# The second dispatch of a mixture-of-experts layer: GpSimd makes its taken blocks, last permutations and expert numbers in place of VectorE, and register loads are moved

## What is computed

```python
x = x + xattn(layernorm(x), ctx)                # W_q, W_kv, W_out, gamma, beta
t = layernorm(x)
probs = softmax(t @ Wg + bg)
top_v, top_i = top_k(probs, 2)                  # two experts per token
top_v = top_v / (top_v.sum() + 1e-6)
for e in range(8):
    h = silu(t @ W1[e] + b1[e]) * (t @ W3[e] + b3[e])      # 128 -> 512
    out = out + combine[..., e] * (h @ W2[e] + b2[e])       # 512 -> 128
x = x + out
```

## Time and profile before

| | before |
|---|---|
| median of 3 runs | 163.03 us (162.93 to 163.41) |
| the profiled execution | 163.78 us, span 161.7 us |
| busy: PE, DVE, ACT, POOL | 136.9, 103.7, 76.2, 75.3 us |
| chain that ended last | PE 66%, DVE 13%, DMA 7%, ACT 7% |

### The profile page before, as it was taken

How to read it: one execution, slowest core, us unless ns; L and a number is a source line. 1 busy time by engine, 2 the same in 40 slices (tenths; PEclk the granted TensorE clock), 3 DMA queues, 4 the chain that set the end, 5 groups by cost and what they waited for, 6 DMA issues and landing times.

```text
span 161.7 us, 3923 instructions
## 1 busy us (share of the span) xinstructions
PE 136.9 (85%) x1152; PEld 128.4 (79%) x1152; DVE 103.7 (64%) x324; ACT 76.2 (47%) x210; POOL 75.3 (47%) x93
## 2 busy tenths in 40 slices
PE   6788896999999999897899899999999999993000
PEld 6677785779998999886778799999999999992000
DVE  0536699989899967988769744535363544444084
ACT  3078356857464698700633335363544545363000
POOL 3630002946553685104810777777777763334000
PEclk9999999999999999999999999999999999999755
DMA  4899910020000001338751399888868868001553
GB/s 136 268 329 285 231 33 0 0 114 19 2 2 4 0 0 46 102 99 287 230 152 70 88 323 307 267 243 247 254 195 247 272 212 276 32 27 41 153 140 97
DMA packets 21597, 23.57 MB, mean 146 GB/s; under 512 B 2333, under 2 KB 14457, under 8 KB 21577
## 3 DMA queue, kind: packets, MB, share of 16 engines
q1 hardware_dynamic: 19968, 20.30, 41.9%
q0 software_dynamic: 1440, 2.95, 6.3%
q10 hardware_dynamic: 169, 0.08, 0.2%
HBM read 19.91 MB, written 3.41 MB: 144 GB/s over the span
## 4 chain that ended last, share of the span: by engine, by line
PE 66%; DVE 13%; DMA 7%; ACT 7%; issue 3%; POOL 1%; SPq 1%; ACTq 0%; POOLq 0%; DVEq 0%
PE psum L1261 26%; PE psum L1274 12%; PE psum L1308 8%; PE psum L1290 5%; DMA early<-in_L_xattn_W_kv_dram 4%; PE psum L1037 2%; PE psum L1039 2%; PE psum L1038 2%; DMA y_back<-y_scratch 2%; DVE prob L753 2%; DVE xn L1030 2%; DVE negmax L748 2%; PE psum L1248 2%; ACT g_room L569 2%; DVE x L1027 1%
## 5 line engine op out<-in xcount | busy, mean ns | idle before, releaser
L1261 PE MATMUL psum<-probT,w 128*128 128x128 f32 x368 | 45.5, 276 | 1.7 <-issue 1.1
L987 DVE SCALAR_TENSOR_TENSOR probT<-psum,bias_col,prob 128x128 f32<-128x128 f32 x92 | 26.0, 343 | 29.7 <-ACT prob L667 29.0
L1261 PEld LDWEIGHTS psum<-probT,w 128*128 128x128 f32 x368 | 43.0, 192 | 2.5 <-issue 2.0
L667 ACT ACTIVATE prob<-psum,bias_col 128x128 f32<-128x128 f32 x92 | 26.2, 368 | 36.0 <-PE psum L1261 36.0
L513 POOL DMA_INDIRECT g_room<-xf_scratch,idx x22 | 22.0, 1000 | 22.1 <-DVE idx L963 8.8
L488 POOL TENSOR_TENSOR prob<-prob,rowsum 128x1232 f32<-128x1232 f32 x8 | 18.0, 2249 | 22.6 <-DVE rowsum L744 22.6
L1274 PE MATMUL psum<-w,probT 128*128 x184 | 25.0, 279 | 0.1
L522 POOL DMA_INDIRECT y_scratch<-xnT,out_row x18 | 17.6, 979 | 13.6 <-DVE xnT L996 10.6
L1274 PEld LDWEIGHTS psum<-w,probT 128*128 128x128 f32 x184 | 22.6, 191 | 0.8 <-issue 0.6
L1308 PE MATMUL psum<-vo,probT 128*128 128x128 f32 (+1 forms) x160 | 19.3, 276 | 0.0
L1308 PEld LDWEIGHTS psum<-vo,probT 128*128 128x128 f32 (+1 forms) x160 | 18.5, 192 | 0.0
(11 more groups left out here) (166 smaller groups left out, 180.2 us busy)
## 6 DMA issues: line engine op xcount, KB each, us to landing
w<-in_L_ffn_W_dram SPq DMA_DIRECT2D x54, 256.0 KB, 3.8
early<-in_L_xattn_W_kv_dram SPq DMA_DIRECT2D x2, 512.0 KB, 7.2
y_back<-y_scratch SPq DMA_DIRECT2D x4, 256.0 KB, 3.7
x_sb<-in_x_dram SPq DMA_DIRECT2D x2, 256.0 KB, 5.3
early<-in_L_xattn_W_q_dram SPq DMA_DIRECT2D x1, 512.0 KB, 7.0
early<-in_L_xattn_W_out_dram SPq DMA_DIRECT2D x1, 512.0 KB, 9.5
early<-in_L_ffn_b_dram SPq DMA_DIRECT2D x1, 512.0 KB, 4.8
xf_scratch<-xf SPq DMA_DIRECT2D x2, 256.0 KB, 2.6
```

The costliest lines, as they stand in the source:

```text
L667: act.activation(silu[:, j % 2, c, :], psum[:, 2 * (j % 2), c * P:(c + 1) * P], ACT.Silu, bias=bias_col[:, 0, bass.ds(expert, 1), c]).then ...
L987: dve.scalar_tensor_tensor(out=hT[:, j % 2, c, :], in0=psum[:, 2 * (j % 2) + 1, c * P:(c + 1) * P], scalar=bias_col[:, 1, bass.ds(expert[j ...
L1261: ins = pe.matmul(psum[:, 2 * (j % 2) + a, c * P:(c + 1) * P], w13[:, j % WR, a, c * P:(c + 1) * P], xt[:, j % XR, :], start=True, stop=True)
```

## The change

POOL takes over four pieces. `taken_blocks` becomes 11 steps ahead of gather(1), each waiting for the one before, and `gone_blocks` 4 steps between gather(2) and gather(3); `last_perm` (2 steps) and `other_experts` (8 steps) stand between gather(4) and gather(5). They leave DVE, which waits for `taken_ok` ahead of `other_tiles`. DVE loads expert number 0 ahead of the first `idx` and numbers 1 to 4 between `gated(0)` and `other_tiles`; `out_row` is made later, behind `bias_down(1)`. PE loads its number between the halves of `up(j)`, and does `logits(2)` ahead of `up(0)`.

```diff
+            def taken_blocks():
...
+                step(pool.tensor_scalar(room_left[:, :], bounds[:, 0, :], -1.0, float(FULL * P), ALU.mult, ALU.add))
+                step(pool.tensor_scalar(room_left[:, :], room_left[:, :], 0.0, None, ALU.max))
+                step(pool.tensor_tensor(taken_e[:, :], blocks[:, :], room_left[:, :], ALU.subtract))
...
+                step(pool.tensor_tensor(taken_of[:, :], pair_taken[:, :, 0], pair_taken[:, :, 1], ALU.add))
+            def gone_blocks():
+
+                pool.wait_ge(perm_ok, 2)
+                step(pool.tensor_copy(floor_2[:, 0:FIRST * K], first_floors))
+                step(pool.tensor_tensor(gone[:, :], floor_2[:, 0:FIRST * K], taken_of[:, :], ALU.subtract))
+                step(pool.tensor_scalar(gone[:, :], gone[:, :], 0.0, float(2 * NT * P), ALU.is_lt, ALU.mult))
+                pool.tensor_tensor(floor_2[:, 0:FIRST * K], floor_2[:, 0:FIRST * K], gone[:, :], ALU.add).then_inc(taken_ok, 1)
...
+                pool.wait_ge(q_ok, 1)
+                pool.tensor_tensor(perm[:, pairs, :],
+                                   iota_q[:, :].rearrange("p (o q) -> p o q", o=1).broadcast_to([P, (T - FIRST) * K, P]),
+                                   q_of[:, FIRST:T, :].rearrange("p t (k o) -> p (t k) o", o=1).broadcast_to([P, (T - FIRST) * K, P]),
+                                   ALU.subtract).then_inc(p_perm, 1)
+                pool.wait_ge(p_perm, 1)
+                pool.tensor_scalar(perm[:, pairs, :], perm[:, pairs, :], 0.0, None, ALU.is_equal).then_inc(perm_2_ok, 1)
+
...
+                pool.wait_ge(base_ok, 1)
+                pool.tensor_tensor(end_e[:, :], base[0:1, :], padded[0:1, :], ALU.add).then_inc(p_eid, 1)
+                pool.wait_ge(p_eid, 1)
+                pool.tensor_tensor(end_e[:, :], end_e[:, :], taken_e[0:1, :], ALU.add).then_inc(p_eid, 1)
...
+                                   ALU.subtract).then_inc(p_eid, 1)
...
+                pool.tensor_scalar(ended[:, :, :], ended[:, :, :], 0.0, None, ALU.is_ge).then_inc(p_eid, 1)
+                pool.wait_ge(p_eid, 4)
...
+                pool.tensor_tensor(eid_f[:, FULL:NT], ended[:, :, 0], ended[:, :, 1], ALU.add).then_inc(p_eid, 1)
+                pool.wait_ge(p_eid, 7)
+                pool.tensor_scalar(eid[:, FULL:NT], eid_f[:, FULL:NT], float(E - 1), None, ALU.min).then_inc(eid_ok, 1)
...
+            taken_blocks()
             for j in range(1, AHEAD):
                 if j == 2:
                     rstd_step(TWICE + G - 1)
+                elif j == 3:
+                    gone_blocks()
+                elif j == FULL:
+                    last_perm()
+                    other_experts()
                 gather(j)
...
+                ins = dve.tensor_tensor(val[:, g.start:g.stop, :], row_of[:, g.start:g.stop, :], q_of[:, g.start:g.stop, :],
+                                        ALU.subtract)
+                if n < 2:
+                    link(ins)
+                else:
+                    ins.then_inc(q_ok, 1)
+                    dve.wait_ge(q_ok, 1)
...
-            def taken_blocks():
...
+                dve.wait_ge(taken_ok, 1)
...
-                link(dve.tensor_reduce(base[:, :], low_pad[:, :, :], AX.X, ALU.add))
+                dve.tensor_reduce(base[:, :], low_pad[:, :, :], AX.X, ALU.add).then_inc(base_ok, 1)
+                dve.wait_ge(base_ok, 1)
...
-            def other_experts():
...
+            expert = {}
+
+            def load_expert(j):
+
+                if j == FULL:
+                    dve.wait_ge(eid_ok, 1)
+                expert[j] = dve.value_load(eid[0:1, j:j + 1], min_val=0, max_val=E - 1)
+
+            dve.wait_ge(eid_1_ok, 1)
+            load_expert(0)
             dve.wait_ge(idx_1_mm, 1)
...
-            taken_blocks()
...
             def gated(j):
 
-                if j == FULL:
-                    dve.wait_ge(eid_ok, 1)
-                expert[j] = dve.value_load(eid[0:1, j:j + 1], min_val=0, max_val=E - 1)
+                if j >= FULL:
+                    load_expert(j)
...
             gated(0)
+            for j in range(1, FULL):
+                load_expert(j)
             other_tiles()
-            one_hots(2)
             gated(1)
             other_rows()
-            other_experts()
             bias_down(0)
...
+                if j == 2:
+                    other_out_rows()
...
-                        pe.wait_ge(perm_ok, 2 if t == 0 else 3)
+                        pe.wait_ge(*((perm_ok, 2) if t == 0 else (perm_2_ok, 1)))
...
-            def up(j, between=None):
-
-                if j == FULL:
-                    pe.wait_ge(eid_ok, 1)
-                expert[j] = pe.value_load(eid[0:1, j:j + 1], min_val=0, max_val=E - 1)
+            def up(j):
...
-                    if a == 0 and between is not None:
-                        between()
+                    if a == 0:
+                        if j == FULL:
+                            pe.wait_ge(eid_ok, 1)
+                        expert[j] = pe.value_load(eid[0:1, j:j + 1], min_val=0, max_val=E - 1)
...
-            up(0, lambda: logits(2))
+            logits(2)
+            up(0)
```

More of the change, by code:

```diff
@@ L234, in build @@
         own_ok = sem("own_ok")
+        p_taken = sem("p_taken")
+        taken_ok = sem("taken_ok")
+        q_ok = sem("q_ok")
+        base_ok = sem("base_ok")
+        perm_2_ok = sem("perm_2_ok")
+        p_eid = sem("p_eid")
+        p_perm = sem("p_perm")
         idx_1_mm = sem("idx_1_mm")
@@ L523, in scatter, with over_pairs, step @@
                                         y_sb[:, j % YR, :], None).then_inc(y_st[j % YR], 16)
+            def over_pairs(ap, n):
+                return ap.rearrange("p (o e) -> p o e", o=1).broadcast_to([P, n, E])
+            first_floors = floor_i[:, 0:FIRST, :].rearrange("p t k -> p (t k)")
+            first_masks = mask[:, 0:FIRST, :, :].rearrange("p t k e -> p (t k) e")
+            steps = [0]
+            def step(ins):
+                ins.then_inc(p_taken, 1)
+                steps[0] += 1
+                pool.wait_ge(p_taken, steps[0])
@@ new lines, in other_experts @@
+            def other_experts():
+                pool.wait_ge(base_ok, 1)
+                pool.tensor_tensor(end_e[:, :], base[0:1, :], padded[0:1, :], ALU.add).then_inc(p_eid, 1)
+                pool.wait_ge(p_eid, 1)
+                pool.tensor_tensor(end_e[:, :], end_e[:, :], taken_e[0:1, :], ALU.add).then_inc(p_eid, 1)
+                pool.wait_ge(p_eid, 2)
+                pool.tensor_tensor(ended[:, :, :], iota_j[0:1, FULL:NT].rearrange("p (j o) -> p j o", o=1).broadcast_to([1, NT - FULL, E]),
+                                   end_e[:, :].rearrange("p (o e) -> p o e", o=1).broadcast_to([1, NT - FULL, E]),
+                                   ALU.subtract).then_inc(p_eid, 1)
+                pool.wait_ge(p_eid, 3)
+                pool.tensor_scalar(ended[:, :, :], ended[:, :, :], 0.0, None, ALU.is_ge).then_inc(p_eid, 1)
+                pool.wait_ge(p_eid, 4)
+                for n, half in enumerate((4, 2)):
+                    pool.tensor_tensor(ended[:, :, 0:half], ended[:, :, 0:half], ended[:, :, half:2 * half], ALU.add).then_inc(p_eid, 1)
+                    pool.wait_ge(p_eid, 5 + n)
+                pool.tensor_tensor(eid_f[:, FULL:NT], ended[:, :, 0], ended[:, :, 1], ALU.add).then_inc(p_eid, 1)
+                pool.wait_ge(p_eid, 7)
+                pool.tensor_scalar(eid[:, FULL:NT], eid_f[:, FULL:NT], float(E - 1), None, ALU.min).then_inc(eid_ok, 1)
@@ L824, in blocks_of @@
                                        ALU.subtract))
-                link(dve.tensor_tensor(val[:, g.start:g.stop, :], row_of[:, g.start:g.stop, :], q_of[:, g.start:g.stop, :],
-                                       ALU.subtract))
+                ins = dve.tensor_tensor(val[:, g.start:g.stop, :], row_of[:, g.start:g.stop, :], q_of[:, g.start:g.stop, :],
[5 more added lines that the diff above has]
+                    dve.wait_ge(q_ok, 1)
             def one_hots(n, g=None):
@@ L920, in other_tiles @@
                                   ALU.mult).then_inc(hit_ok, 1)
-            def other_experts():
-                link(dve.tensor_tensor(end_e[:, :], base[0:1, :], padded[0:1, :], ALU.add))
-                link(dve.tensor_tensor(end_e[:, :], end_e[:, :], taken_e[0:1, :], ALU.add))
-                link(dve.tensor_tensor(ended[:, :, :], iota_j[0:1, FULL:NT].rearrange("p (j o) -> p j o", o=1).broadcast_to([1, NT - FULL, E]),
-                                       end_e[:, :].rearrange("p (o e) -> p o e", o=1).broadcast_to([1, NT - FULL, E]), ALU.is_ge))
-                link(dve.tensor_reduce(eid_f[:, FULL:NT], ended[:, :, :], AX.X, ALU.add))
-                dve.tensor_scalar(eid[:, FULL:NT], eid_f[:, FULL:NT], float(E - 1), None, ALU.min).then_inc(eid_ok, 1)
             def other_rows():
@@ L971, in _ @@
             blocks_of(2)
-            dve.wait_ge(eid_1_ok, 1)
             dve.wait_ge(ld["bias"], 16)
-            expert = {}
```

(5 more changed lines are left out.)

21 lines of the change are left out of this document (11 added, 10 removed).

## The result

| | before | after |
|---|---|---|
| median, same chip | 163.22 us (162.93 to 164.05) | 166.69 us (165.28 to 167.69) |
| ratio | | 1.0188, interval 1.0146 to 1.0230 |
| profiled execution, span | 163.78, 161.7 us | 166.40, 164.6 us |
| busy: PE, DVE, POOL | 136.9, 103.7, 75.3 us | 137.8, 101.0, 84.2 us |

The forecast was 163.1 us with a range up to 164.2. The busy times moved as the change intends (2.7 us off DVE, 8.9 us onto POOL), and the time rose by 3.5 us all the same.

What follows compares the result with a forecast made beforehand. PE bounds the steady expert loop, so only the start of up(4) can move. `idx` +0.37, behind it -0.5 and POOL +0.25 make +0.1 us on the median of 163.03: 163.1 us, range 162.2 to 164.2.

Steps and rivals of the forecast that it cites:

- POOL's eight steps: Second dispatch's expert numbers on POOL ahead of gather(5): 3.15 us from 85.7, done at 88.85.
- gather(5) 0.25 us behind what `idx` allows: POOL and `idx` tie ahead of gather(5); +0.25 us taken for DVE's `tile_hit` operations holding POOL.
- The one-hots off DVE: Last group's permutation leaves DVE between `other_tiles` and `idx`: some 0.6 us less, 3.67 for 4.27.
- Behind `idx`: From xT(5) to up(4): 1.01 to 1.1 us in place of 1.59, a gain of 0.5 us.
- No load inside up(j) shows past 95 us: PE's load in the middle of up(j) costs nothing; PE gaps there past 95 us would prove the forecast wrong.
- POOL holds gather(5): Slower rival, chance 0.30: POOL's eight expert steps, held beside DVE, delay gather(5) by 0.92 to 1.15 us; 163.8 to 164.0 us.
- 88.4 to 89.7: Sign of being wrong: gather(5) starting outside these times; it was expected near 89.1.
- The ranks come at about 80.5 in place of 80.09: +0.4 us: Last group's ranks on PE, with logits ahead of up(0) and the first load's 0.3 included; bounds +0.2 and +0.6.
- the load's +0.3 us: Register load 0 on DVE ahead of the first `idx` delays it to 74.1, and `direct_xT` behind it; bounds +0.05 and +0.4.
- costed at nothing: `taken_blocks` on POOL: eleven steps, 4.0 us, done at 74.0, just before the `idx` that gather(1) waits for.
- Four loads of 0.6 follow one another: DVE's loads 1 to 4 ahead of `other_tiles`: 3.0 us in place of 2.45, `other_tiles` at 84.8, +1.0 us.
- A change of it enters one for one as long as PE has slack: Any change on the line from ranks over `idx` and gather(5) to xT(5) moves the end by its own size.

Runs made afterwards that it cites:

- e12: Kernel before with DVE's load 0 behind the last direct add, load 1 behind the last group's top two, PE's loads inside up(j): 162.43 us, 0.9921; again 162.89 us, 0.9961.
- e13: The change with the second dispatch's expert numbers back on DVE, behind `other_rows`: 164.71 us, 1.0071 of the kernel before.
- e1: The change with the load of expert number 0 put back in front of gated(0): 167.36 us, 1.0214 of the kernel before.
- e2: The change with 14 in place of 8 warm-up transposes ahead of `direct_xT`: 165.95 us, 1.0149 of the kernel before.
- e3: The change with loads 1 to 4 back at the head of their gated(j): 165.10 us, 1.0078 of the kernel before.
- e6: The kernel before with 3 in place of 8 warm-up transposes ahead of `direct_xT`: 163.50 us, 1.0002.
- e11: The change's moved loads and logits alone, all of POOL's new work on DVE as before: 165.65 us, 1.0117 of the kernel before.
- e10: POOL's part of the change alone, loads and logits where they stood in the kernel before: 164.06 us, 1.0034.
- e7: The change with load 0 behind `add_direct(7)`, load 1 behind `top_two(2)`, loads 2 to 4 in gated(j), expert numbers still on POOL: 165.10 us, 1.0033.
- e14: The change with load 0 behind `add_direct(7)`, load 1 behind `top_two(2)`, loads 2 to 4 in gated(j), second expert numbers on DVE: 162.05 us, 0.9893.

## Why the prediction was wrong, point by point

**Right, with their sizes.** POOL's eight steps: 3.15 us forecast, 3.16 measured (87.62 to 90.78). gather(5) 0.25 us behind what `idx` allows: +0.25; but that size is luck. I had put it for DVE holding POOL's steps up, and they took 3.16 us for 3.15; what held gather(5) are 0.42 us between POOL's last step and the gather, for which I had 0.15. The one-hots off DVE: -0.60 forecast between `other_tiles` and `idx`, -0.47 measured. Behind `idx`: -0.5 forecast, -0.40 measured; of the two reasons that I gave, PE's load and the expert numbers off DVE, PE's load is enough: e12 and e13 have the same 1.19 us from xT(5) to up(4) with the expert numbers on DVE. No load inside up(j) shows past 95 us. The rival 'POOL holds gather(5)' named the right place but the wrong price: it was held 0.25, not 0.92 to 1.15. gather(5) started at 91.20, outside the 88.4 to 89.7 that I had named as the sign of being wrong.

**The step that failed most: "The ranks come at about 80.5 in place of 80.09: +0.4 us".** They came 2.21 later. I had carried the load's +0.3 us through `direct_xT` as a delay and nothing else; no case of mine asked what PE's clock does behind a longer wait. It fell to half for three microseconds: +1.31 in `direct_xT`, 1.51 up to the ranks. In e1 and e2, where PE's idle time there is short, the clock stays up and the term is gone; in e3, with 0.76 us of it, the term is there again. In e6, e11 and e13 it is not, with 0.73 to 0.87 us: the fall came only behind a longer wait, but not behind each, and what decides it stays open. The load itself cost 0.86 us on DVE (forecast 0.83). The other 0.2 of the 0.60 at the first `idx` came from `taken_blocks` on POOL, which I had costed at nothing: beside it `key_in` took 0.25 us, and 0.16 in e12, where POOL is idle there. POOL's part without the load (e10) put the first `idx` back by 0.11.

**"Four loads of 0.6 follow one another": mis-sized.** From `val` to `other_tiles` I had 3.0 us and it took 3.48. The rows give 2.84 us from the first load to `floor` in place of 2.4, and one piece of 0.39 "issue" between the first load and the second makes the difference. I had also written that these places are idle only if something else keeps DVE waiting there and that no row shows it; that sentence was right, and it should have carried the forecast: e12 with two loads at better places is 0.8% faster than before, about half of it by DVE's loads: the same kind of move with the opposite sign.

**Missing: gather(5) itself.** I had followed gather(5) to its start and taken its 2.57 us over unchanged. Making the expert numbers at the same time as the row list also releases SP's weight loads at the same time. In the six kernels in which POOL makes the expert numbers ahead of gather(5) (the change, e1, e2, e3, e7, e10), its start to xT(5) is 3.3 to 3.7 us. In the kernels in which DVE makes them behind `idx` it is 2.5 to 2.7 (3.0 in e11, where PE at half clock and not the rows held xT(5)). SP asks for the next weights 0.5 to 0.7 us behind gather(5) in those six and 2.2 to 2.4 behind it in all others. That the place decides is shown by e13 against the change and by e14 against e7; that it is the weight loads beside it which slow the gather is argued from their start and wasn't tried by itself.

**The path beyond the forecast's slack.** "A change of it enters one for one as long as PE has slack" fails in the same way three times more: in e1, e7 and e11 a wait of PE of 1.8 to 2.5 us cost more than its length, since what followed ran at 1.2 GHz.

## What to carry to other kernels

When a change lengthens the wait of a matmul engine, look at its granted clock behind that wait, and give the half clock a case and a price in the forecast: here, for about half a microsecond more of waiting, 1.3 us in the change and e3, and nothing in e6, e11 and e13. A register load, or any small step, is free only in a wait that the timeline shows, and only up to that wait's length; behind the last input of the critical path it costs its full 0.6 us. When a value is made earlier, list every queue that it releases: the expert numbers were ready in time, and their weight loads went out beside the gather that PE waited for.
